# Attention and mixture-of-experts layer: four split-weight slots, W1 split a tile ahead, products grouped by kind, some up-products ahead of the router

## The reference

```python
x = x + attn(layernorm(x))      # additive attention: softmax over tokens per head, pooled query and key
x = x + ffn(layernorm(x))
# ffn:
normed = h * rsqrt(mean(h*h) + 1e-8) * norm_weight
shared = relu(normed @ sw1 + sb1) @ sw2 + sb2             # 256 -> 1024 -> 256, every token
scores, idx = top_k(sigmoid(normed @ router_w.T), 2)      # of 8 experts
w = scores / (sum(scores) + 1e-6)
routed = sum over the 2 chosen e of w_e * (relu(normed @ ew1[e] + eb1[e]) @ ew2[e] + eb2[e])
return shared + routed
```

## Time and profile before

| | |
|---|---|
| median of 3 runs | 828.69 us (827.51 to 830.9) |
| the profiled execution | 826.31 us, its span 824.5 us |
| mean granted TensorE clock | 0.969 |
| busy, share of the span | TensorE 91%, weight loads 75%, DVE 69%, ACT 54%, GpSimd 22% |
| DMA | 106.8 MB, 130 GB/s over the span |

### The profile page before, as it was taken

The page is one execution under the profiler, slowest core; times in us unless marked ns, Lnnn a source line. Parts: engine busy times, 40 slices in busy tenths (PEclk is TensorE's granted clock), DMA queues, the critical chain, the costliest instruction groups (busy, mean ns, idle before and its releaser), DMA issues. The chain is left out here.

```text
span 824.5 us, 11746 instructions
## 1 busy us (share of the span) xinstructions
PE 752.6 (91%) x4254; PEld 620.0 (75%) x4254; DVE 570.5 (69%) x1179; ACT 442.8 (54%) x739; POOL 185.0 (22%) x163
## 2 busy tenths in 40 slices
PE   3588998888998999989989989989999989998987
PEld 3345665567886889879878979878888979897776
DVE  6633666589576568666775767666766767677995
ACT  3541134535533764665847485755857485747332
POOL 2200111000000404332523334442433332220000
PEclk9878999799999999999999999999999999999999
DMA  9200012100050234462634564452744564333860
GB/s 331 109 1 2 26 64 74 42 1 0 1 211 1 64 115 160 145 236 84 240 143 145 169 235 149 155 196 102 255 151 144 183 224 151 116 135 107 279 200 32
DMA packets 45657, 106.80 MB, mean 130 GB/s; under 512 B 9277, under 2 KB 33600, under 8 KB 37920
## 3 DMA queue, kind: packets, MB, share of 16 engines
q1 hardware_dynamic: 38784, 88.36, 30.9%
q0 software_dynamic: 6816, 17.71, 6.5%
HBM read 89.26 MB, written 17.69 MB: 130 GB/s over the span
## 5 line engine op out<-in xcount | busy, mean ns | idle before, releaser
L712 PE MATMUL psD<-w,hhi 128*128 128x512 f32 x824 | 301.1, 406 | 16.2 <-DVE x_sb L1160 11.9
L867 ACT ACTIVATE hid<-psU,b 128x512 f32<-128x512 f32 (+2 forms) x280 | 153.5, 576 | 248.9 <-issue 172.9
L713 PE MATMUL psD<-w,hlo 128*128 128x256 f32 x824 | 233.0, 283 | 0.0
L692 PE MATMUL psU<-xhl,w 128*128 128x512 f32 (+2 forms) x560 | 194.9, 348 | 15.7 <-DVE w L1166 13.9
L1137 DVE TENSOR_TENSOR hlo<-hid,hhi 128x512 fp32r<-128x512 f32 x206 | 141.1, 691 | 91.8 <-ACT hhi L870 89.3
L712 PEld LDWEIGHTS psD<-w,hhi 128*128 128x128 f32 x824 | 156.4, 190 | 58.6 <-DVE x_sb L1160 13.8
L693 PE MATMUL psU<-xhl,w 128*128 128x512 f32 (+2 forms) x560 | 194.8, 348 | 0.0
L694 PE MATMUL psU<-xhl,w 128*128 128x512 f32 (+2 forms) x560 | 194.3, 347 | 0.0
L713 PEld LDWEIGHTS psD<-w,hlo 128*128 128x128 f32 x824 | 156.3, 190 | 0.2
L397 POOL DMA_INDIRECT xin<-token_in,src x71 | 79.1, 1115 | 297.2 <-PE psT L668 154.2
L692 PEld LDWEIGHTS psU<-xhl,w 128*128 128x128 f32 x560 | 106.9, 191 | 32.4 <-DVE w L1166 16.1
(11 more groups left out here) (196 smaller groups left out, 607.3 us busy)
## 6 DMA issues: line engine op xcount, KB each, us to landing
raw<-in_wpack SPq DMA_DIRECT2D x30, 1024.0 KB, 7.8
xT<-in_wpack SPq DMA_DIRECT2D x28, 1024.0 KB, 7.2
xT<-token_out SPq DMA_DIRECT2D x32, 256.0 KB, 4.4
x_sb<-in_x SPq DMA_DIRECT2D x8, 512.0 KB, 9.3
token_in<-z_sb SPq DMA_DIRECT2D x8, 512.0 KB, 2.9
out<-x_sb SPq DMA_DIRECT2D x16, 256.0 KB, 4.7
b<-in_b2pack SPq DMA_DIRECT2D x29, 128.0 KB, 3.6
att<-in_attn SPq DMA_DIRECT2D x1, 1379.0 KB, 11.5
```

Source lines behind the costliest of these rows:

```text
L692: mm(acc, whi[:, slot, col], xhl[:, k, 0, 0:rows], start=(k == 0), stop=False)
L712: mm(acc, hhi[:, part], w[:, slot, :, col], start=(c == 0), stop=False)
L713: last = mm(acc[:, 1, :], hlo[:, part], whi[:, slot, col], start=False, stop=(c == MH - 1))
L867: last = nc.scalar.activation(hid[:, n % 4, i * rows:(i + 1) * rows], acc, ACT.Relu, bias=b1[:, u % 2, m:m + 1])
```

## The change

Split weights get a fourth slot `w3`, laid over the part of `xT` that is dead after the fourth shared tile; matrix h of weights u has slot (2u + h) % 4. Raw matrices have two buffers, one for each h, each loaded again when its predecessor has been split. `xT` is stored by tile. W1 of u+1 is split a group ahead, behind W2 of u, on ACT and on DVE; in group 4 both W1 halves of the first expert come ahead of row 0. `up` computes, for each bank, the two products of high weights and xhi, the two of low weights, and then the two with xlo, and waits for xhi at its start and for xlo before the last two of its first bank; `down` computes the eight hhi products of 128 rows (waiting for hhi) and then the eight hlo products. Chunks 0 to 3 of up(0) stand between the last transposes, the router and the logits' transposes; the logits are transposed into psT. The bias of the shared rows comes from a buffer of its own, `b2s`, and is added for all 32 rows behind the A tiles.

```diff
+        with ExitStack() as experts:
+            w3 = experts.enter_context(nc.sbuf_tensor("w3", [P, 2, W2], F32R))
+        xT = sb("xT", [P, SH, KD, 512])
...
+        wpair = [w[:, 0], w[:, 1], w[:, 2], w3]
+        whi, wlo = ([pair[:, i, :] for pair in wpair] for i in range(2))
+        b2s = sb("b2s", [P, D])
...
-        raws = [raw[:, 0, :], raw[:, 1, :], xT[:, 0, 0:W2], xT[:, 1, 0:W2]]
...
             def matrix(u, h, e):
-                r = (2 * u + h) % 4
-                if u >= 2:
-                    sp.wait_ge(w_lo[h], u - 1)
+                if u >= 1:
+                    sp.wait_ge(w_lo[h], u)
...
-                sp.dma_start(raws[r], src[:, h * W2:(h + 1) * W2]).then_inc(raw_loaded[r], 16)
+                sp.dma_start(raw[:, h, :], src[:, h * W2:(h + 1) * W2]).then_inc(raw_loaded[h], 16)
...
             sp.wait_ge(routed, 1)
             e = expert_id(0)
-            sp.wait_ge(xlo_ready, W2 // 512)
             matrix(1, 0, e)
             matrix(1, 1, e)
             biases(1, e)
             e = expert_id(1)
             matrix(2, 0, e)
-            matrix(2, 1, e)
             for j in range(SLOTS):
                 g, u = SA + j, j + 1
+                matrix(u + 1, 1, e)
+                if u + 2 <= SLOTS + 1:
+                    after = expert_id(j + 2) if j + 2 < SLOTS else E
+                    matrix(u + 2, 0, after)
                 sp.wait_ge(out_done, Q0[g])
-                biases(u + 1, expert_id(j + 1) if j + 1 < SLOTS else E)
-                if j + 2 <= SLOTS:
-                    e = expert_id(j + 2) if j + 2 < SLOTS else E
-                    matrix(u + 2, 0, e)
-                    matrix(u + 2, 1, e)
+                biases(u + 1, e)
+                e = after
...
+            def up(g, slot, groups=None):
+                pe.wait_ge(xhi_ready, g + 1)
...
+                        for k in range(KD):
+                            mm(acc, whi[slot][:, cols[k]], xhl[:, k, 0, 0:rows], start=(k == 0), stop=False)
+                        for k in range(KD):
+                            mm(acc, wlo[slot][:, cols[k]], xhl[:, k, 0, 0:rows], start=False, stop=False)
+                        if j == 0 and i == 0:
+                            pe.wait_ge(xlo_ready, g + 1)
+                        for k in range(KD):
+                            last = mm(acc, whi[slot][:, cols[k]], xhl[:, k, 1, 0:rows], start=False, stop=(k == KD - 1))
...
+            def down(g, slot):
...
+                    for c in range(MH):
+                        if q == 0 and c * rows % 512 == 0:
+                            if nrow[g] == 4:
+                                pe.wait_ge(hid_ready, G0[g] + c + 1)
+                            else:
+                                pe.wait_ge(hhi_ready, casts[g] + c * rows // 512 + 1)
+                        part = slice(c * rows + q * P, c * rows + (q + 1) * P)
+                        mm(acc, hhi[:, part], wpair[slot][:, :, c * D:(c + 1) * D], start=(c == 0), stop=False)
+                    for c in range(MH):
+                        if q == 0 and c * rows % 512 == 0:
+                            pe.wait_ge(hlo_ready, G0[g] + c * rows // 512 + 1)
...
+                        last = mm(acc[:, 1, :], hlo[:, part], whi[slot][:, col], start=False, stop=(c == MH - 1))
...
-            for c in range(4, NC + 2):
+            for c in range(4, NC + 1):
...
+            pe.wait_ge(w_lo[0], 1)
+            pe.wait_ge(x1_ready, NT // 2)
+            up(0, 0, (0, 1))
+            turn_chunk(NC - 1)
+            up(0, 0, (2,))
             router(1)
+            up(0, 0, (3,))
+            pe.wait_ge(zT_ready, NT // 2)
...
-                up(g, 2 * u % 3)
+                up(g, 2 * u % 4, range(4, 8) if g == 0 else None)
...
                 z_out(2 * c + 1)
                 if c == NC // 2:
                     logits_out(0)
+                if c == NC - 2:
+                    turned_hi(0)
             logits_out(1)
...
                 if g + 1 < NG and use[g + 1] > use[g]:
                     u = use[g + 1]
-                    act.wait_ge(down_done, Q0[g])
-                    split_hi(0, u, 2 * u % 3)
-                    split_hi(1, u, (2 * u + 1) % 3)
+                    if g == SA - 1:
+                        split_hi(0, u, 2 * u % 4)
+                        act.wait_ge(xlo_ready, RING)
+                    else:
+                        act.wait_ge(down_done, Q0[g])
+                    split_hi(1, u, (2 * u + 1) % 4)
+                    if u + 1 <= SLOTS + 1:
+                        act.wait_ge(up_ps, G0[g + 1])
+                        split_hi(0, u + 1, 2 * (u + 1) % 4)
...
                 normalise_chunk(c - 1)
+            turned_lo(0)
...
                 if kinds[g] == "S":
                     row = x_sb[:, 4 * nth[g] + q, :]
-                    dve.wait_ge(b_loaded[u % 2], 32 * (u // 2 + 1))
-                    V.tensor_tensor(row, row, b2[:, u % 2, :], ALU.add).then_inc(bias_added, 1)
+                    if g > SA:
+                        dve.wait_ge(bias_added, NT)
...
                 if nrow[g] == 4:
+                    if g == SA - 1:
+                        half_lo(0, u, 0)
+                        half_lo(0, u, 1)
                     out_rows_of(g, 0)
                     if fresh:
-                        half_lo(0, u, 0)
+                        half_lo(1, u, 0)
                     out_rows_of(g, 1)
                     if fresh:
-                        half_lo(0, u, 1)
+                        half_lo(1, u, 1)
                     out_rows_of(g, 2)
-                    if fresh:
-                        half_lo(1, u, 0)
-                        half_lo(1, u, 1)
+                    if ahead:
+                        half_lo(0, u + 1, 0)
+                        half_lo(0, u + 1, 1)
                     out_rows_of(g, 3)
+                    if kinds[g] == "A":
+                        shared_bias(nth[g])
                 else:
-                    half_lo(0, u, 0)
-                    half_lo(0, u, 1)
+                    half_lo(1, u, 0)
+                    half_lo(1, u, 1)
                     for q in range(nrow[g]):
                         out_rows_of(g, q)
-                    half_lo(1, u, 0)
-                    half_lo(1, u, 1)
+                    if ahead:
+                        half_lo(0, u + 1, 0)
+                        half_lo(0, u + 1, 1)
...
+            def shared_bias(i):
...
+                for t in range(3 * i, min(NT, 3 * i + 3)):
+                    V.tensor_tensor(x_sb[:, t, :], x_sb[:, t, :], b2s[:], ALU.add).then_inc(bias_added, 1)
```

More of the change, by code:

```diff
@@ L590, in turn_chunk, with ranks, turn @@
                 turn_z(2 * c + 1)
+            def ranks():
+                pe.wait_ge(onehot_ready, 1)
+                ohf = oh[:].rearrange("p t e -> p (t e)")
+                mm(psD[:, 1, 0:NT * E], tri, ohf, start=True, stop=True)
+                mm(psD[:, 1, NT * E:2 * NT * E], ones, ohf, start=True, stop=True).then_inc(rank_ps, 1)
+            def turn(j):
+                pe.wait_ge(xin_loaded[j % 2], 16 * rows_of_side[j])
+                if j == 0:
+                    pe.wait_ge(idx_ready, 1)
+                for q in range(nrow[SA + j]):
+                    for k in range(KD):
+                        last = nc.tensor.transpose(psT[:, k, q * P:(q + 1) * P], xin[:, j % 2, q, k * P:(k + 1) * P], ident)
+                last.then_inc(blkT_ps, 1)
@@ new lines, in down @@
+            def down(g, slot):
+                rows = nrow[g] * P
+                for q in range(nrow[g]):
+                    n = Q0[g] + q
+                    if n >= 2:
+                        pe.wait_ge(out_done, n - 1)
+                    if n == 1:
+                        pe.wait_ge(rank_read, 1)
+                    acc = psD[:, n % 2, :].rearrange("p (s n) -> p s n", s=2)
+                    for c in range(MH):
[9 more added lines that the diff above has]
+                            pe.wait_ge(hlo_ready, G0[g] + c * rows // 512 + 1)
+                        part = slice(c * rows + q * P, c * rows + (q + 1) * P)
+                        col = slice(c * D, (c + 1) * D)
+                        last = mm(acc[:, 1, :], hlo[:, part], whi[slot][:, col], start=False, stop=(c == MH - 1))
+                    last.then_inc(down_done, 1)
+                    if g == FIND:
+                        find(2 + q)
+                    if g == FIND + 1 and q >= 2:
+                        find(4 + q)
@@ L797, in logits_out, with turned_hi @@
                 nc.scalar.activation(lgT[:, r, :], psD[:, r, :], copy).then_inc(logits_sb, 1)
+            def turned_hi(g):
+                rows = nrow[g] * P
+                if kinds[g] == "S":
+                    if g:
+                        act.wait_ge(up_ps, G0[g])
+                    else:
+                        act.wait_ge(z_stored[0], 32)
+                    for k in range(KD):
+                        last = nc.scalar.activation(xhl[:, k, 0, :], xT[:, nth[g], k, :], copy)
```

(8 more changed lines are left out.)

155 lines of the change are left out of this document (49 added, 106 removed).

## The result

The kernel after took 794.34 us (793.84 to 796.28, 4 runs) against 829.40 (827.51 to 830.90, 4 runs) for the kernel before beside it: a ratio of 0.9583, 95% interval 0.9556 to 0.9609. Two executions that took far longer than all others (1458.97 us, the kernel before beside some variants; 2815.25 us, one of the variant order_old, whose median still counts it) are left out of the ratios. The profiled execution took 793.84 us with a span of 792.1; before it was 826.31 and 824.5.

The account below looks back on a forecast made before the run. TensorE sets the pace in the expert tiles, DVE at entry and tail. Terms -13.0 - 5.1 - 1.5 - 0.3 + 0.8 - 7.0 = -26.1 from 826.31 give 800.2, plus 2.4 to the median: 802.6 us; range 795 to 813.

Parts of the forecast that it names:

- Part 2: New order of products in up- and down-stages: 1.5 us gained, all in C tiles' down-stages, no change of rate.
- I take 0: Down-stages: the new order changes no product rate, because hhi products keep their two-piece moving operand; 0 us.
- Parts 3 and 4: Entry: early up-products and moved bias adds together -0.3 us, between -1 and +2.
- Rival 4: A tiles' down-stages: the order pays, each pair losing its 0.29 us per A tile; 795.1 us, chance 0.12.
- Stagger and clock: Behind C tiles: six waits for split W1 go, -13.0 us; three half-clock stretches after such waits go, -5.1.
- The rival of late raws: Two raw buffers too few: loads take 10 us or more, half of each C-tile wait stays; 811.8 to 814, chance 0.13.
- Kind by kind: Down-stage with hhi products before hlo: C tiles wait less for hlo, 6 x 0.25 = -1.5 us; rate unchanged.
- its bound of 7.5 us: Most the down-stage order could gain if every pair lost its 0.29 us: 0.29 x 824/32 = 7.5 us.
- part 3: Entry: twelve up-products of tile 0 ahead of the router delay DVE's routing, +3.3 us.
- part 4: Shared rows' bias adds moved off DVE's path: -2.6 us up to the stall near 201, -1.0 at two waits.
- Tile 4: DVE splits W1 before tile 4's first output row, so the row comes late: +0.8 us.
- Tail: Last up-stage starts earlier, -2.5 us; eight rows without bias adds, -4.2; hhi ahead of hlo, -0.3; together -7.0.

Follow-up runs that it names:

- order_old: Kernel after with both product orders undone (up products in triples, down products in pairs), stagger and bias kept: 802.63 us, ratio 0.9695.
- ctl_after: The kernel after itself, run again unchanged as the yardstick beside the variants: 795.10 us, ratio 0.9607.
- down_old: Kernel after with the hhi and hlo products of the down-stage alternating in pairs again: 798.83 us, ratio 0.9660.
- contig: Kernel after with high and low weight halves interleaved by blocks, so an hhi product's 512 moving columns are one piece: 795.49 us, ratio 0.9615.
- bias_old: Kernel after with the shared rows' 32 bias adds just ahead of each row again, as before the change: 805.32 us, ratio 0.9740.
- entry_full: Kernel after with the entry put back: up-products behind the router, xhi and xlo of tile 0 behind the logits: 793.46 us, ratio 0.9605.
- down_mix: Kernel after with each down-stage's first rows ordered by pairs and only its last row kind by kind: 796.24 us, ratio 0.9623.
- wait_filled: stagger_off plus seven unread 512-column products on TensorE in each wait behind a C tile: 811.98 us, ratio 0.9814.
- stagger_off: Kernel after with slots and orders kept, but W1 split in the same tile as W2 again: 816.73 us, ratio 0.9881.
- combo_filled: Kernel after with old entry, tile 4's first row ahead of W1's splits, and unread products in TensorE's three waits before the router: 787.54 us, ratio 0.9517.

## Where the prediction held, and where it failed

The time lies outside the range. Two terms of the sum were mis-sized. Part 2 took nothing for the order's effect on the rate, and nothing for the slots (the sentence "I take 0"): tiles 5 to 30 gained 4.1 us more than predicted. Parts 3 and 4 together were put at -0.3, and measured -2.35. Rival 4 named 795.1, near what came out, but by another mechanism: the A tiles' pairs, whose 0.29 it priced, gained only 0.1 us in all from the order (order_old against ctl_after); its nearness is luck.

**Stagger and clock: right.** The boundaries behind C tiles gave 14.6 us, where 13.0 for the waits and 1.5 for the order were predicted. The A tiles' up-stages gave 5.6, where 5.1 were predicted for three cold stretches; undoing the stagger alone cost 18.4 in tiles 5 to 30. The clock's share is shown by itself: filling the waits gave back 1.6 us for each cold stretch (predicted 1.7). The rival of late raws hardly appeared. Loads landed in

```profile
DMA to landing us min/median/max: 5.0/5.5/11.3
```

and ACT waited for one twice: 5.6 us in tile 4, predicted and without effect, and 1.1 us at a C tile behind a B tile (467.29), where the room was put at 6.3 us.

**Kind by kind: the sentence "I take 0" failed.** The C tiles' term, 1.5 us, was right (6 x 0.25 in down_old). Beside it the prediction compared the pair's spacing with that of two runs and argued that the two-piece operand would keep the hhi products slow. The operand costs nothing (contig), and the A tiles' down-stages, the largest part of what its bound of 7.5 us was for, gained 1.4 us in all, nearly all of it with the slots. The larger gain lay in a stage for which the text took no change: 8 x 0.21 us in the B tiles' up-stages. Together the order was worth 4.2 us in the middle (order_old) and not 1.5, the slots 1.4 and not 0. That is the 4.1 us between -19.6 and -23.73. (With the stagger's 18.4 the three make 24.0, 0.3 more than was measured; undoing one part at a time shares such remainders out in no fixed way.)

**The entry: each part right, their sum wrong.** The routing on DVE starts 20.31 us behind the last projection in the kernel after, and 17.83 in the one before: 2.5 later, just short of the predicted 2.7 to 4.0. Each part alone is seen from the last projection to tile 4, before at 132.55: part 3 without part 4 (bias_old) 135.65, +3.1 (predicted +3.3); part 4 without part 3 (entry_full) 129.10, -3.5 (predicted -3.6). Together they should have left it at 132.2, and it is 130.20. The 2 us go with cold stretches: 13.6 us at half clock between 141 and 261 us after (6.8, 3.4, 3.4), 20.4 before and in entry_full, 23.8 in bias_old. Most of it shows at the routing. In the nine traces of variants that keep the entry and the up order of the kernel after (itself three times), the routing starts 20.3 us behind the last projection where the first cold stretch lasts 6.8 us (five traces), and 21.7 to 21.8 where it lasts 10.2 (contig, down_mix, wait_filled, bias_old). So part 3 cost 3.9 in bias_old and 2.5 in the kernel after: 1.4 of the 2 us. Contig and down_mix keep that delay and start tile 4 at 131.84 and 131.78; wait_filled has it too, but no cold stretch near 260, and stands at 130.24. The up-products ahead of the router fill a part of TensorE's time at the lower clock, and the clock can come back among them: the prediction named that for the start of the routing (early or late) and then summed the middle, +3.3. Which of the two comes differs between executions with the same TensorE order there, so that all three profiled executions of the kernel after had the early one is in part luck. That filled waits save 5.7 us at the entry shows the size to be well within what the clock can do; that the missing stretches make the remaining 0.6 too is argued from these traces.

**Tile 4: right** (+0.69, predicted +0.8; 0.88 by undoing it). **Tail: mechanism right, 1.0 too large**: the up-stage came 2.23 earlier and not 2.5, and the rest gave 3.8 and not 4.5; the bias rows by themselves are 3.5.

**Outside the change**: the stretch ahead of the last projection was 1.05 shorter, which is scatter, and 2.4 us were put between the profiled execution and the median where it was 0.5 this time. These 2.9 us, the order and slots (4.1), the entry (2.05), tile 4 (0.1) less the tail's 1.0 make 8.2 of the 8.3 us missed.

## What to carry to other kernels

Double-buffer what is derived (split weights), and not only what is loaded, where the short tiles come: the raw buffers can be fewer if the derivation runs a stage ahead. Where TensorE must wait some 2 us, look at the granted clock behind the wait; a few products that nobody reads, into a bank that is free, may be worth having where the wait can't be shortened, and here they gave the best version. Be slow to move work ahead of the step that feeds the bounding engine: here it cost 1.2 us at tile 4, and the median shows no gain.

## What the runs showed of the hardware

- A run of 48 products of 256 columns keeps one of two spacings, 0.118 or 0.1133 us each, and the kind of products ahead of it chooses. Why is open.
- The same 64 products of an A tile's down-stage take 11.19, 11.30 or 11.39 us by the slot that holds the weights and the order; with the new order (slots 3 and 1) they take 11.30 and 11.2, with pairs 11.19 and 11.39. That it is the address is argued; slots and everything else that alternates by tile were not separated, though the kernel before alternates its inputs too and shows one length.
- Waits of 2.0 to 2.3 us were enough for 3.4 us at a granted clock of 0.50, in three of seven cases in the kernel before and in three of seven in stagger_off; filled with products, in none. The other four of seven leave no trace, and which ones do changes with the timing; even a wait of 3.46 us left none in combo_filled.
- Loads of a raw matrix landed in a median of 5.5 us in the kernel after, where almost all were issued one at a time. In the kernel before two were issued together, and landed in a median of 6.0 (the first) and 8.4 (the second); the 7.8 of the earlier trace rows is that of the half of them whose buffer bears the name raw.
